# Attention probabilities: 32 by 32 blocks on VectorE and a round trip through device memory in place of transposes on TensorE

## The reference

```python
q = apply_rope((query @ wq).reshape(bs, sq, 32, 128).transpose(0, 2, 1, 3), pos)
k = apply_rope(repeat((key @ wk).reshape(bs, sk, 8, 128), 4), pos)
scores = einsum('bhqd,bhkd->bhqk', q, k) / scale
attn = softmax(scores + m[:, None, :, :], axis=-1)
out = einsum('bhqk,bhkd->bhqd', attn, v)
return out.transpose(0, 2, 1, 3).reshape(bs, sq, 32 * 128) @ wo
```

## Time and profile before

| what | value |
| --- | --- |
| median of 3 runs | 1836.22 us (1835.92 to 1838.24) |
| the profiled execution | 1838.36 us, its span 1836.5 us |
| granted TensorE clock, mean | 0.998 |
| TensorE busy | 1812.3 us (99%) |
| VectorE, ScalarE, GpSimd busy | 1108.9, 666.6, 609.4 us |
| moved by DMA | 190.72 MB, mean 104 GB/s |

### The profile page before, as it was taken

One profiled execution on the slowest core, in us unless ns is written; L12 is line 12 of the kernel. 1 busy time (PEld: TensorE's weight loads), 2 busy tenths in 40 slices (PEclk: granted clock), 3 DMA queues, 4 the chain that ended last, 5 costly groups with the idle time before them and its releaser, 6 DMA issues.

```text
span 1836.5 us, 27785 instructions
## 1 busy us (share of the span) xinstructions
PE 1812.3 (99%) x9672; PEld 1651.7 (90%) x9672; DVE 1108.9 (60%) x2498; ACT 666.6 (36%) x1371; POOL 609.4 (33%) x428
## 2 busy tenths in 40 slices
PE   7999999999999999999999999999999999999998
PEld 6999999999888888889999998899999999999986
DVE  7631365656433333346666668877777778787755
ACT  5211210103323232231110114666656666565634
POOL 3223531226222222212222233444435344353514
PEclk9999999999999999999999999999999999999999
DMA  4112342345433333323222234332323323232223
GB/s 139 58 57 70 140 124 82 114 132 176 147 123 123 124 123 123 106 75 128 91 101 102 91 130 128 99 97 77 105 75 103 85 84 105 64 105 88 72 74 111
DMA packets 138531, 190.72 MB, mean 104 GB/s; under 512 B 42704, under 2 KB 109392, under 8 KB 137536
## 3 DMA queue, kind: packets, MB, share of 16 engines
q1 hardware_dynamic: 138432, 189.45, 33.1%
HBM read 142.49 MB, written 46.92 MB: 103 GB/s over the span
## 4 chain that ended last, share of the span: by engine, by line
PE 82%; DVE 2%; POOL 2%; DMA 2%; ACT 1%; issue 1%; SPq 0%; DVEq 0%; ACTq 0%; POOLq 0%
PE bank L195 74%; PE bank L1877 4%; POOL shared_operand_low L314 1%; PE bank L101 1%; PE bank L2147 1%; DMA aw_weights_then_ctx_rows<-in_wk 1%; PE bank L181 1%; PE bank L2160 1%; DMA aw_weights_then_ctx_rows<-in_wv 1%; DVE e_scores L1630 1%; POOL w_rest_low L779 1%; DVE e_scores L1610 0%; DMA ctx_raw<-in_ctx_t 0%; PE bank L1272 0%; PE bank L1269 0%
## 5 line engine op out<-in xcount | busy, mean ns | idle before, releaser
L195 PE MATMUL bank<-shared_operand_high,w_first_high 128*128 128x448 f32 (+1 forms) x768 | 280.4, 365 | 1.3 <-DVEq L795 0.7
L195 PE MATMUL bank<-shared_operand_low,w_first_high 128*128 128x448 f32 (+1 forms) x768 | 279.3, 364 | 0.0
L195 PE MATMUL bank<-shared_operand_high,w_first_low 128*128 128x448 f32 (+1 forms) x768 | 279.3, 364 | 0.0
L1621 ACT ACTIVATE e_scores<-e_scores,e_nmax 112x375 f32<-112x375 f32 x256 | 155.8, 616 | 121.8 <-DVE e_nmax L1614 116.5
L314 POOL TENSOR_TENSOR shared_operand_low<-ctx_raw,shared_operand_high 128x768 fp32r<-128x768 f32 x64 | 119.6, 1882 | 196.4 <-ACT shared_operand_high L310 196.4
L195 PEld LDWEIGHTS bank<-shared_operand_high,w_first_high 128*128 128x128 f32 x768 | 145.2, 189 | 12.9 <-POOL w_first_low L486 1.0
L195 PEld LDWEIGHTS bank<-shared_operand_high,w_first_low 128*128 128x128 f32 x768 | 145.3, 189 | 11.6
L195 PEld LDWEIGHTS bank<-shared_operand_low,w_first_high 128*128 128x128 f32 x768 | 145.4, 189 | 11.0
L1411 POOL TENSOR_TENSOR w_first_low<-aw_weights_then_ctx_rows,w_first_high 128x1024 fp32r<-128x1024 f32 x30 | 71.9, 2398 | 224.1 <-ACT w_first_high L1393 224.1
L1610 DVE CUSTOM_DVE_ANT_0 e_scores<-bank,e_mask_then_layer_ffn 112x375 f32<-112x375 f32 x256 | 139.8, 546 | 9.6 <-PE bank L1877 0.4
L1591 POOL TENSOR_TENSOR e_v_low<-e_raw_v,e_v_high 128x384 fp32r<-128x384 f32 x64 | 65.1, 1018 | 228.5 <-ACT e_v_high L1580 228.5
(11 more groups left out here) (253 smaller groups left out, 4462.8 us busy)
## 6 DMA issues: line engine op xcount, KB each, us to landing
ctx_raw<-in_ctx_t SPq DMA_DIRECT2D x64, 384.0 KB, 3.8
e_raw_wo<-in_wo SPq DMA_DIRECT2D x32, 512.0 KB, 4.9
aw_weights_then_ctx_rows<-in_wq SPq DMA_DIRECT2D x30, 512.0 KB, 3.6
q_rotated<-q_rotated_then_x_rows SPq DMA_DIRECT2D x64, 224.0 KB, 1.9
e_raw_q<-q_rotated SPq DMA_DIRECT2D x64, 224.0 KB, 2.8
v_rows<-v_out SPq DMA_DIRECT2D x48, 256.0 KB, 2.3
e_raw_v<-v_rows SPq DMA_DIRECT2D x64, 192.0 KB, 3.3
k_rotated<-k_rotated_sb SPq DMA_DIRECT2D x64, 188.0 KB, 1.9
```

What stands on the lines that cost most here:

```text
L195: mm = pe.matmul(out, stationary[a], moving[b], start=(first and i == 0), stop=(last and i == 2))
L1621: act.activation(self.s_buf[:, t, h, 0:KEYS], self.s_buf[:, t, h, 0:KEYS], ACT.Exp, bias=self.nm[:, t, h:h + 1], accum_out=self.total[:, t ...
```

## The change

The 12 transposes on TensorE go. Instead VectorE transposes 32 by 32 blocks of the normalised probabilities in two instructions of two heads each (128 partitions by 768 elements); SyncE writes the result (128 by 6144 bytes) to device memory in one transfer, `carry_out`, and reads it back in four, `carry_in`, each into 32 partitions (512 runs of 1536 bytes in all), so that the blocks come to stand in transposed places. Queries are laid out in four blocks of 28 padded to 32, so the scores have 128 partitions in place of 112. The four heads of scores now have a bank each, and the output two banks in turn.

Scores and mask are negated (the queries' rotation table on the host, the mask once on ScalarE), so that the minimum that the masking pass returns is at once the bias of the exponential; the four small negations of the maximum (line 1614) go. Two of the four normalisations move from VectorE to ScalarE, two of the three low parts of the probabilities from VectorE to GpSimd. High and low parts are now made from the copy in SBUF and not from PSUM.

Everything runs further ahead: scores three steps ahead (steps 0 to 2 within `query1_phase`), block transposes and the round trip two steps ahead, queries and keys loaded six steps ahead. Buffers are laid out anew, the constants share one semaphore, and the last stage's down weights take the room of the raw queries. In the diff below the lines that the step bodies lose are left out where the list above tells them.

```diff
-LOWEST = -3.4028234663852886e38
+HIGHEST = 3.4028234663852886e38
+BLOCK, BLOCKS = 32, 4
+QUERIES = SEQ // BLOCKS
...
+    p_dram = nc.dram_tensor("probabilities", (2, P, BLOCKS, PER_GROUP * KEY_TILES * BLOCK), F32, kind="Internal").ap()
...
+                if i == LAST - 2 and t == 1:
+                    first.carry_out(sp, 0)
+                    first.carry_in(sp, 0)
+                if i == LAST - 1:
+                    if t == 0:
+                        first.load_v(sp, 0, 0, 0)
+                        first.load_qk(sp, 4, 4, 0)
+                        first.load_v(sp, 1, 1, 0)
+                    else:
+                        first.carry_out(sp, 1)
+                        first.carry_in(sp, 1)
+                        first.load_qk(sp, 5, 5, 0)
...
+        i, unit = LAST - 2, 4 * (LAST - 2)
+        rotated_half(dve, unit, i, 0, 0)
+        first.mask_scores(dve, 0, 0, range(PER_GROUP))
+        rotated_half(dve, unit + 1, i, 0, 1)
+        first.invert(dve, 0, 0)
+        first.normalise(dve, 0, 0, (0, 1))
+        first.transpose(dve, 0, 0, (0, 1))
+        rotated_half(dve, unit + 2, i, 1, 0)
+        first.transpose(dve, 0, 0, (2, 3))
+        first.mask_scores(dve, 1, 1, range(PER_GROUP))
+        rotated_half(dve, unit + 3, i, 1, 1)
+        i, unit = LAST - 1, 4 * (LAST - 1)
+        first.invert(dve, 1, 1)
+        first.normalise(dve, 1, 1, (0, 1))
+        rotated_half(dve, unit, i, 0, 0)
+        first.transpose(dve, 1, 1, (0, 1))
+        first.transpose(dve, 1, 1, (2, 3))
+        rotated_half(dve, unit + 1, i, 0, 1)
+        first.mask_scores(dve, 2, 2, range(PER_GROUP))
+        rotated_half(dve, unit + 2, i, 1, 0)
+        rotated_half(dve, unit + 3, i, 1, 1)
...
-            if not (known(s) and s < 1 and h < 2):
-                pe.wait_ge(self.masked, 4 * s + h - 1)
-            split_product(pe, self.s_bank[h % 2][0:SEQ, 0:KEYS_EVEN], [x[:, t, h, :] for x in self.q],
+            if s >= 1:
+                pe.wait_ge(self.masked, 4 * s - 4 + h + 1)
+            split_product(pe, self.s_bank[h][:, 0:KEYS_EVEN],
+                          [x[:, t, h].rearrange("p i b -> p (i b)") for x in self.q],
                           [x[:, t, :] for x in self.kt], True, True).then_inc(self.scored, 1)
     def mask_scores(self, dve, s, u, heads):
         t = u % 2
         for h in heads:
             dve.wait_ge(self.scored, 4 * s + h + 1)
-            if not (known(s) and s < 2):
-                dve.wait_ge(self.turned, 3 * s - 3)
+            if s >= 2:
+                dve.wait_ge(self.transposed, 2 * s - 2)
             take_waits(dve, self.k.passed)
-            dve.tensor_tensor_reduce(self.s_buf[:, t, h, 0:KEYS], self.s_bank[h % 2][0:SEQ, 0:KEYS], self.mask[:, u, :],
-                                     1.0, LOWEST, ALU.add, ALU.max,
-                                     self.mx[:, t, h:h + 1]).then_inc(self.masked, 1)
-            dve.wait_ge(self.masked, 4 * s + h + 1)
-            dve.tensor_scalar(self.nm[:, t, h:h + 1], self.mx[:, t, h:h + 1], -1.0, None,
-                              ALU.mult).then_inc(self.negated, 1)
+            dve.tensor_tensor_reduce(self.s_buf[:, t, h, 0:KEYS], self.s_bank[h][:, 0:KEYS], self.mask[:, u, :],
+                                     1.0, HIGHEST, ALU.add, ALU.min,
+                                     self.least[:, t, h:h + 1]).then_inc(self.masked, 1)
     def exps(self, act, s, u, heads):
         t = u % 2
         for h in heads:
-            act.wait_ge(self.negated, 4 * s + h + 1)
-            act.activation(self.s_buf[:, t, h, 0:KEYS], self.s_buf[:, t, h, 0:KEYS], ACT.Exp, bias=self.nm[:, t, h:h + 1],
+            act.wait_ge(self.masked, 4 * s + h + 1)
+            act.activation(self.s_buf[:, t, h, 0:KEYS], self.s_buf[:, t, h, 0:KEYS], ACT.Exp,
+                           bias=self.least[:, t, h:h + 1], scale=-1.0,
                            accum_out=self.total[:, t, h:h + 1]).then_inc(self.exped, 1)
-    def normalise(self, dve, s, u):
+    def invert(self, dve, s, u):
         t = u % 2
         dve.wait_ge(self.exped, 4 * s + 4)
         dve.reciprocal(self.inv[:, t, :], self.total[:, t, :]).then_inc(self.inverted, 1)
+    def normalise(self, dve, s, u, heads):
+        t = u % 2
         dve.wait_ge(self.inverted, s + 1)
-        for h in range(PER_GROUP):
-            dve.tensor_scalar(self.s_buf[:, t, h, 0:KEYS], self.s_buf[:, t, h, 0:KEYS], self.inv[:, t, h:h + 1], None,
-                              ALU.mult).then_inc(self.normed, 1)
+        for h in heads:
+            dve.tensor_scalar(self.s_buf[:, t, h, 0:KEYS], self.s_buf[:, t, h, 0:KEYS], self.inv[:, t, h:h + 1],
+                              None, ALU.mult).then_inc(self.normed, 1)
+    def normalise_last(self, act, s, u):
+        t = u % 2
+        act.wait_ge(self.inverted, s + 1)
+        for h in (2, 3):
+            act.activation(self.s_buf[:, t, h, 0:KEYS], self.s_buf[:, t, h, 0:KEYS], ACT.Copy,
+                           scale=self.inv[:, t, h:h + 1]).then_inc(self.last_normed, 1)
+    def transpose(self, dve, s, u, heads):
+        t, h = u % 2, heads[0]
+        if h == 0:
+            dve.wait_ge(self.normed, 2 * s + 2)
+            if s >= 2:
+                dve.wait_ge(self.shuffled[t], 64 * (s // 2))
+        else:
+            dve.wait_ge(self.last_normed, 2 * s + 2)
+        take_waits(dve, self.k.passed)
+        piece = KEY_TILES * BLOCK
+        dve.transpose(self.in_blocks[:, t, :, h * piece:(h + 2) * piece].rearrange("p j (m k) -> p m j k", k=BLOCK),
+                      self.s_buf[:, t, h:h + 2, :].rearrange("p h (c j k) -> p (h c) j k", j=BLOCKS, k=BLOCK)
+                      ).then_inc(self.transposed, 1)
+    def carry_out(self, sp, s):
+        t = s % 2
+        sp.wait_ge(self.transposed, 2 * s + 2)
+        if s >= 2:
+            sp.wait_ge(self.shuffled[t], 64 * (s // 2))
+        sp.dma_start(self.k.p_dram[t], self.in_blocks[:, t]).then_inc(self.carried, 16)
+    def carry_in(self, sp, s):
+        t = s % 2
+        sp.wait_ge(self.carried, 16 * s + 16)
+        if s >= 2:
+            sp.wait_ge(self.pt_low_first, s - 1)
+            sp.wait_ge(self.pt_low, 2 * s - 2)
+        for j in range(BLOCKS):
+            sp.dma_start(self.pt_raw[t][BLOCK * j:BLOCK * (j + 1)],
+                         self.k.p_dram[t, :, j].rearrange("(i a) x -> a i x", i=BLOCKS)).then_inc(
+                self.shuffled[t], 16)
...
+    def negate_mask(self, act):
+        act.wait_ge(self.mask_in, 16)
+        act.activation(self.mask, self.mask, ACT.Copy, scale=-1.0).then_inc(self.padded, 1)
...
-            if s == STEPS - BATCH - 3:
+            if s == STEPS - BATCH - 6:
                 for q_stored in first.q_stored:
                     sp.wait_ge(q_stored, 16 + 16 * HEADS // 2)
-            if s + 3 < STEPS:
-                first.load_qk(sp, s + 3, (u + 3) % 8, g + (u + 3) // 8)
+            if s + 2 < STEPS:
+                first.carry_out(sp, s + 2)
+            if s + 6 < STEPS:
+                first.load_qk(sp, s + 6, (u + 6) % 8, g + (u + 6) // 8)
             if s + 2 < STEPS:
                 first.load_v(sp, s + 2, (u + 2) % 8, g + (u + 2) // 8)
             if g == 0 and u == 1:
...
             if 1 <= s <= FILLED:
                 last_heads.store(sp, s - 1)
-        for q_stored in first.q_stored:
-            sp.wait_ge(q_stored, 16 + 16 * (HEADS // 2 - 1))
+            if s + 2 < STEPS:
+                first.carry_in(sp, s + 2)
...
+        def take_output(s):
+            u = s % BATCH
+            act.wait_ge(o_acc, s + 1)
+            act.activation(o_columns(ot[0][u // 4], u), by_block(o_banks[s % 2][:, 0:HALF]),
+                           ACT.Copy).then_inc(o_high, 1)
         def step(s, u, g):
+            if s >= 1:
+                take_output(s - 1)
             if s + 2 < STEPS:
+                first.normalise_last(act, s + 2, u)
+            act.wait_ge(first.shuffled[s % 2], 64 * (s // 2) + 64)
             for c in range(KEY_TILES):
+                act.activation(by_block(pt[0][:, c, :]), raw_p(s, c), ACT.Copy).then_inc(pt_high, 1)
+            if s + AHEAD < STEPS:
+                first.exps(act, s + AHEAD, u + AHEAD, (0, 1))
+            if s + 5 < STEPS:
+                first.qk_high_part(act, s + 5, u + 5)
+            if s + AHEAD < STEPS:
+                first.exps(act, s + AHEAD, u + AHEAD, (2, 3))
+            if s + 1 < STEPS:
+                first.v_high_part(act, s + 1, u + 1)
+            if wo_tile(u, g) is not None:
                 split_wo(s, u, g)
         steps(act, step)
+        take_output(STEPS - 1)
...
+            for c in (1, 2):
+                pool.wait_ge(pt_high, 3 * s + c + 1)
+                pool.tensor_tensor(by_block(pt[1][:, c, :]), raw_p(s, c), by_block(f32(pt[0][:, c, :])),
+                                   ALU.subtract).then_inc(pt_low, 1)
+            if s + 5 < STEPS:
+                first.qk_low_part(pool, s + 5, u + 5)
+            if s + 1 < STEPS:
```

(62 more changed lines are left out.)

334 lines of the change are left out of this document (149 added, 185 removed).

## The result

The change makes the kernel slower: 2008.12 us, median of 4 runs (1999.18 to 2013.69), against 1836.83 us for the kernel before, a ratio of 1.0927 [1.0884, 1.097]. The forecast was 1766 us with a range to 1825.

What follows compares the result with a forecast made beforehand. TensorE alone was taken to bound the kernel. From 1838.4 us, 73.6 for transposes and 4.5 for early waits came off, 1.5 for the end and 6 for contention were added: 1767.8, or 1766 against the median; range 1752 to 1825.

Steps and rivals of the forecast that it cites:

- The step that failed: SyncE's queue: round trip's latency covered by two steps; only loads six steps ahead stand behind the wait for the write.
- Rival 3: Round trip slower in both directions, below 228 GB/s, kernel slower than before; 1916 us at 195 GB/s; chance 0.13.
- Rival 4: The chain through six hand-offs waits on itself somewhere and gives all of the gain back; 1836 us; chance 0.02.
- steps above 9 us with neither engine full nor DMA late: Profile sign in the attention steps that would show the prediction wrong in mechanism; no price given.
- the two for the ends: First and last attention steps: 4.5 us gained from early waits, 1.5 us lost in the last three steps.
- TensorE's floor: TensorE's attention step without the transposes: 9.95 - 1.15 = 8.8 us.
- the 128 stationary columns: Scores on TensorE with 128 stationary columns for 112: claimed to cost nothing.
- The block transpose: New VectorE operation, two a step of 768 elements: 0.94 us each, bounds 0.6 to 1.9 us.
- the sum of 1766: Whole kernel: all terms summed to 1767.8 us against the profiled execution, 1766 against the median of the runs.
- I take that it just fits: DMA engines: round trip's 4.9 us and loads' 3.1 us make 8.0 of a step's 8.8 us.
- rival 2: DMA engines become the bound through slow reads into 32 partitions, still a gain; 1790 to 1825 us; chance 0.19.
- Contention: VectorE held up by GpSimd in SBUF: waits of 1 to 3 us a step, priced at 0.1 a step, 6 us.

Runs made afterwards that it cites:

- early_loads_last: wo_early with the loads of queries, keys and values issued behind the reads of the probabilities; 1876.81 us, ratio 1.0205.
- early_in_one: wo_early with the four reads made one read into 128 partitions, blocks not brought to their places; 1768.85 us, ratio 0.9622.
- wo_early: wo_first with the weight loads spread, issued one to four steps ahead of their use, partly in plain steps; 1779.46 us, ratio 0.9685.
- wo_first: The changed kernel with the weight load moved to the head of the same SyncE step, ahead of the write; 1799.82 us, ratio 0.9789.
- loads_first: The changed kernel with all four loads of a step issued ahead of the write; 1877.85 us, ratio 1.0213.

## Why the prediction was wrong

**The step that failed** is one sentence of the round trip: "SyncE waits for the write to land before it issues the read; behind that stand only loads that now run six steps ahead." It is false twice. The weight load stands there too, and it is used in the same step; moving it ahead removes 208 us. And the loads of queries and keys are six steps ahead only in their index: they are issued about a step before ScalarE reads them, as early_loads_last shows; those of the values are two ahead even by index. Besides, that sentence looked at the wait for the landing alone. The larger one is the wait for the block transposes at the head of SyncE's step, 346.3 us in 52 times against 70.3 for the landing. The text worked out when the probabilities would be there and never when each load behind them would be. The cost went off the path that was examined and came in over a queue.

**The rivals.** Rival 3 had the sign, by a mechanism that the runs exclude: the write landed in 4.2 us and half of the reads brought 12 us. Rival 4, a chain that waits on itself somewhere, was the mechanism; the prediction gave it 0.02, let it give back exactly the gain, and said that nothing in the rows points to it. Something in the diff did: a wait on VectorE's late work at the head of a list that holds a load of the same step. The sign "steps above 9 us with neither engine full nor DMA late" was named and is half met: no engine is full, but one transfer is late, the weight tile, because it is issued late. The text had no price for it.

**What held.** With the loop gone, most terms can be read; the two for the ends (4.5 gained, 1.5 lost) were not read by themselves. TensorE's floor is 8.8 us in a step (8.7 to 8.8 in plain steps of the changed kernel, 8.78 in early_in_one), so the 128 stationary columns cost nothing, as the earlier trace rows said. The block transpose takes 0.969 us where 0.94 was forecast by 1 ns an element. VectorE was busy 7.4 to 7.5 us in a plain step (7.0 forecast). The write landed in 4.2 us (4.3 forecast), each read in 4.9 (4 to 7), and the DMA share of plain steps was 0.88 and 0.97 (0.85 to 0.95). early_in_one, at 1768.85 us, is near the sum of 1766: with one read in place of four and the tiles loaded early, the steps are those of the forecast. It is another kernel than the one forecast, though, since its blocks do not come to their places; the nearest that computes the whole is wo_early, 13 us above the sum.

**What was mis-sized.** "I take that it just fits": it does in plain steps, while the weight steps of wo_first, which load 512 KB more, take 10.15 us, and its DMA share is 0.98 from 1250 to 1650 us. At 0.46 us a step, the 56 steps of groups 1 to 7 make 26 us of the 34 between the forecast and wo_first, whose 1799.82 us lie inside rival 2. It is not the sum of bytes that does not fit: early_in_one moves the same bytes in steps of 8.78 us, at a share of 0.91, with one read into 128 partitions. What was missing is a term for the form and the place of the transfers: four reads of 32 partitions, and the weight load right behind them. The Trainium skill ("SBUF — State Buffer", section "Door 1: The DMA port swizzle") gave an estimate of 9.8 us and 1820 for rival 2. By that rule 32 partitions occupy the engines longer for the same bytes, and the shares 0.98 and 0.88 agree; but the time that it cost here is 5.6 us, and the number of transfers in the queue counted for more.

**Contention** was priced at 6 us. The waits are there and cost nothing that can be found. The normalisations and the low part of the first tile, ns shortest/median/longest:

```profile
L1706 DVE TENSOR_SCALAR e_scores<-e_scores,e_inv x128: 406/876/2640, 1097.7 to 1906.1; 128x375 f32<-128x375 f32 x128
...
L1977 DVE TENSOR_TENSOR e_p_t_low<-e_shuffled,e_p_t_high x32: 624/1292/1581, 1146.0 to 1920.7; 128x448 fp32r<-128x448 f32 x32
```

Against their shortest, two of the first a step at a mean of 895 ns and one of the second lose some 1.6 us, within the 1 to 3 that were worked out. That GpSimd is what holds them up is read from single cases and no run takes it apart: the normalisation of 1.06 us from 1440.42 in the changed kernel ended 0.2 us behind GpSimd's operation of 1440.26 to 1441.28. In early_in_one the first still have a median of 704 ns against 406 at their shortest, and its steps are 8.78 us: VectorE is busy 0.85 of the time there, so the waits fit under TensorE.

## What to carry to other kernels

When a change puts a wait into an engine's list, write down every instruction behind it up to the end of that step, and for each its first consumer; if the next of these waits depends on that consumer, even over other engines, the step becomes the sum of the loop. A load's lead is set by its first reader, its buffers and its place in the queue, not by the index in its call. Where the printed chain names a releaser, hold it against the wait in the kernel and against the times. When several engines are idle in the same kind of step and busy in the others, look for a loop through a DMA queue before bandwidth.

## What had not been expected of the hardware

The granted clock fell in the weight steps to 0.79 and 0.87 on average, between its two levels of 1.2 and 2.4 GHz, where TensorE had stood idle for 6 to 7.6 of some 17 us; in plain steps between them it was 1.00. TensorE's busy time in such a step was 10.1 to 11.0 us for 8.8, which adds to its busy time but not to the loop, in which no matmul stands. The issue of a transfer on SyncE can take longer behind the write: the key load (line 1622), 0.51 us in the earlier trace rows, took 1.03 us as median where it is the second issue behind the write (wo_first; 1.02 in early_in_one) and 0.51 where it is not (loads_first, early_loads_last). The load between them, line 1619, kept a median of 0.43 in all four, so the reason is open. And a write of 768 KB issued behind other loads held up SyncE for up to 8.8 us (loads_first), where the longest wait was 2.4 us in the changed kernel and 3.9 in wo_first.
